# A transformer program on one core: a new table of TensorE's side jobs, and the transposed probabilities fetched by three DMAs of 12 blocks instead of two of 18

## The reference, cut to what matters

```python
# third layer: causal attention, 32 query heads, 8 key/value heads, head size 64, rope
xq = (x @ wq).reshape(Bx, Tx, N_HEAD, HEAD_DIM)
xk = (x @ wk).reshape(Bx, Tx, N_KV_HEAD, HEAD_DIM)
xv = (x @ wv).reshape(Bx, Tx, N_KV_HEAD, HEAD_DIM)
xq = xq * cos + _rotate_half(xq) * sin
xk = xk * cos + _rotate_half(xk) * sin
scores = jnp.einsum('bqhd,bkhd->bhqk', xq, xk) * scale
scores = jnp.where(causal[None, None], scores, -jnp.inf)
probs = jax.nn.softmax(scores, axis=-1)
out = jnp.einsum('bhqk,bkhd->bqhd', probs, xv)
return out.reshape(Bx, Tx, N_HEAD * HEAD_DIM) @ wo
```

## Time and profile before

| | |
|---|---|
| median of 2 runs | 609.65 us (608.51 to 610.8) |
| the profiled execution: its own time | 610.31 us |
| the profiled execution: its span, first to last instruction | 608.5 us |
| granted TensorE clock, mean over the span | 0.992 |
| PE busy | 557.9 us (92%) |
| ACT busy | 436.8 us (72%) |
| DVE busy | 458.2 us (75%) |
| POOL busy | 452.5 us (74%) |
| share of the 16 DMA engines taken by the hardware queue of SP | 82.1% |

### The profile page before, as it was taken

How to read it: one execution, slowest core, us unless ns; L and a number is a source line. 1 busy time by engine, 2 the same in 40 slices (tenths; PEclk the granted TensorE clock), 3 DMA queues, 4 the chain that set the end, 5 groups by cost and what they waited for, 6 DMA issues and landing times.

```text
span 608.5 us, 16334 instructions
## 1 busy us (share of the span) xinstructions
PE 557.9 (92%) x6880; PEld 481.3 (79%) x6880; DVE 458.2 (75%) x751; ACT 436.8 (72%) x608; POOL 452.5 (74%) x371
## 2 busy tenths in 40 slices
PE   5999999987879999999989999999999997996898
PEld 4878898976767898888878888888888976885666
DVE  4686766777767888887877877788788875675897
ACT  0524401249688889889788988988988888974876
POOL 3034426447998998999899899899999977874423
PEclk9999999999999999999999999999999999997989
DMA  8160004006999999999999999999999999998001
GB/s 283 62 209 0 2 21 83 11 2 138 183 175 194 193 183 195 194 199 196 180 181 198 219 196 195 181 212 184 196 177 210 197 184 203 190 177 158 1 27 44
DMA packets 317193, 91.76 MB, mean 151 GB/s; under 512 B 305984, under 2 KB 316224, under 8 KB 317120
## 3 DMA queue, kind: packets, MB, share of 16 engines
q1 hardware_dynamic: 311680, 86.66, 82.1%
q10 hardware_dynamic: 5440, 4.06, 2.6%
HBM read 13.11 MB, written 1.05 MB: 23 GB/s over the span
## 4 chain that ended last, share of the span: by engine, by line
PE 41%; POOL 18%; DVE 16%; DMA 11%; ACT 6%; SPq 4%; issue 4%; POOLq 0%; ACTq 0%; DVEq 0%
POOL p_lo L501 13%; PE PS L1278 12%; DMA pT_lo<-p_lo 10%; PE PS L1537 7%; DVE small L1097 6%; PE PS L1557 4%; PE PS L1411 3%; SPq L402 3%; ACT probs L715 2%; POOL roped L490 2%; PE PS L1388 2%; PE PS L1393 2%; PE PS L1389 2%; PE PS L1301 2%; PE PS L1561 2%
## 5 line engine op out<-in xcount | busy, mean ns | idle before, releaser
L501 POOL TENSOR_TENSOR p_lo<-probs,p_hi 128x2048 f16<-128x2048 f32 (+7 forms) x128 | 303.6, 2390 | 34.4 <-DMA pT_lo<-p_lo 18.8
L715 ACT ACTIVATE probs<-PS,small 128x128 f32<-128x128 f32 (+7 forms) x256 | 173.5, 743 | 43.7 <-DVE small L1097 41.6
L1097 DVE TENSOR_REDUCE small<-PS 128x2 f32<-128x2048 f32 (+7 forms) x128 | 172.8, 1351 | 21.4 <-PE PS L1537 20.9
L724 ACT CAST p_hi<-probs 128x2048 f16<-128x2048 f32 (+7 forms) x128 | 145.8, 1160 | 5.0 <-DMA pT_hi<-p_hi 4.9
L1557 PE MATMUL PS<-v_hi,pT_hi 128*128 128x65 f16 x1152 | 78.8, 194 | 1.3 <-DMA pT_hi<-p_hi 1.3
L1561 PE MATMUL PS<-v_lo,pT_hi 128*128 128x64 f16 x1152 | 78.7, 195 | 0.0
L1537 PE MATMUL PS<-k_hi,q_hi 64*128 64x512 f32 (+3 forms) x384 | 74.0, 381 | 2.5 <-ACT probs L715 2.5
L1557 PEld LDWEIGHTS PS<-v_hi,pT_hi 128*128 128x128 f16 x1152 | 73.9, 99 | 3.0 <-issue 1.4
L1561 PEld LDWEIGHTS PS<-v_lo,pT_hi 128*128 128x128 f16 x1152 | 72.5, 98 | 0.5
L1537 PE MATMUL PS<-k_lo,q_hi 64*128 64x512 f32 (+3 forms) x384 | 66.0, 339 | 0.0
L1537 PE MATMUL PS<-k_hi,q_lo 64*128 64x512 f32 (+3 forms) x384 | 66.0, 339 | 0.0
(11 more groups left out here) (210 smaller groups left out, 1349.6 us busy)
## 6 DMA issues: line engine op xcount, KB each, us to landing
wgu_nat<-L_ffn_w_gate_up SPq DMA_DIRECT2D x2, 1024.0 KB, 9.4
wo_nat<-L_attn_wo ACTq DMA_DIRECT2D x7, 256.0 KB, 3.1
wkq_nat<-L_attn_wq ACTq DMA_DIRECT2D x6, 256.0 KB, 5.1
x<-L_attn_x SPq DMA_DIRECT2D x4, 256.0 KB, 3.9
wdn_nat<-L_ffn_w_down SPq DMA_DIRECT2D x1, 1024.0 KB, 11.0
wfc_nat<-L_ffn_w_fc SPq DMA_DIRECT2D x1, 1024.0 KB, 6.7
wpj_nat<-L_ffn_w_proj SPq DMA_DIRECT2D x1, 1024.0 KB, 9.8
pT_hi<-p_hi SPq DMA_TRANSPOSE x64, 5.5
```

The costliest lines, as they stand in the source:

```text
L501: nc.gpsimd.tensor_tensor(p16_lo[G % 2][:, cols], probs[G % 2][:, cols], p16_hi[G % 2][:, cols], ALU.subtract).then_inc(p_lo_done, 1)
L715: nc.scalar.activation(probs[G % 2][:, start:start + w], PS[:, src:src + w], ACT.Exp, bias=nmax[:, 4 * (G % 2) + u:4 * (G % 2) + u + 1]).t ...
L724: nc.scalar.copy(p16_hi[G % 2][:, cols], probs[G % 2][:, cols]).then_inc(p_hi_done, 1)
L1097: nc.vector.tensor_reduce(nmax[:, first:first + 2], both_heads(G, part), AX.X, ALU.max, negate=True).then_inc(nmax_done, 1)
```

## The change

Three things are changed.

1. The two transposes of a step become three. The float16 probabilities of a step, high and low, now lie in one tile p16 of 36 blocks (high in blocks 0 to 17, low in 18 to 35), the transposed ones in one tile pT of 36 blocks. SP transposes blocks 0 to 11, 12 to 23 and 24 to 35 (`turn_third`). The first third waits for the first part of `p_high` alone when that part has at least 12 blocks (it has 10, 12, 14 or 16), else for both; the second waits for both parts of `p_high` and the first of `p_low`; the third for both of `p_low`. `pv` waits for each third as it comes to its first block. `p_high` of part 0 now waits for the first third of two steps before, and if it has more than 12 blocks for the second as well, `p_high` of part 1 for the second; `p_low` of part 0 waits for the second and the third.
2. The tables. JOBS is new in nearly every step. In a step of groups 1 to 6 the rope projections were 1, 2, 2, 2, 1, 0, 0, 0 and become 1, 2, 1, 1, 1, 2, 0, 0; the output projections were in steps 4, 5, 6, 7 and come to 2, 4, 6, 7, in the order 1, 2, 0, 3, and those of the middle tiles (1, 2) wait for three "ot" jobs, not four; "ot0" moves from step 7 to step 5, "kt1" from slot 2 of step 5 to slot 2 of step 6, "q0t1" to slot 0 of step 7. In RAMP_JOBS "q0t0" moves from step 6 to step 5. The wo weights are split at step 1 of every group but the first, not at step 2 (for the groups before the last).
3. Addresses: roped, y and yT_hi move by 1.5 KB, t_sin by 1.5 KB, o32 to other places, to make room for the joined tiles.

The diff, without the hunks of addresses and of the order count `qk_index`:

```diff
...
-    p16_hi = [sb(f"p16_hi{b}", 186 + 9 * b, [18 * P], F16) for b in range(2)]
-    p16_lo = [sb(f"p16_lo{b}", 190.5 + 9 * b, [18 * P], F16) for b in range(2)]
-    pT_hi = [sb(f"pT_hi{b}", kb, [18, P], F16) for b, kb in enumerate((26, 30.5, 104.5))]
-    pT_lo = [sb(f"pT_lo{b}", kb, [18, P], F16) for b, kb in enumerate((60, 128, 132.5))]
-    o32 = [sb(f"o32{b}", kb, [4, HEAD], F32) for b, kb in enumerate((109.5, 110.5, 78, 79))]
+    p16 = [sb(f"p16_{b}", 186 + 9 * b, [36 * P], F16) for b in range(2)]
+    p16_hi = [t[:, 0:18 * P] for t in p16]
+    p16_lo = [t[:, 18 * P:36 * P] for t in p16]
+    pT = [sb(f"pT_{b}", kb, [36, P], F16) for b, kb in enumerate((26, 128, 104.5))]
...
 
         scores_done, nmax_done, exp_done = sem("scores_done"), sem("nmax_done"), sem("exp_done")
         p_hi_done, p_lo_done = sem("p_hi_done"), sem("p_lo_done")
-        pT_hi_landed = [sem(f"pT_hi_landed{b}") for b in range(3)]
-        pT_lo_landed = [sem(f"pT_lo_landed{b}") for b in range(3)]
+        pT_landed = [[sem(f"pT_third{k}_landed{b}") for b in range(3)] for k in range(3)]
         pv_done, recip_done, norm_done = sem("pv_done"), sem("recip_done"), sem("norm_done")
         oT_done, oT_hi_done, oT_lo_done = sem("oT_done"), sem("oT_hi_done"), sem("oT_lo_done")
         wo_done = sem("wo_done")
...
 
             return {NT - 2: 0, NT - 1: 2}.get(t, 4)
 
+        THIRD = 12
+
+        def third_landed(k, G):
+
+            return pT_landed[k][G % 3], 16 * (G // 3 + 1)
+
         def q_tile(G, part):
             return blocks(G, part) - 1
 
...
 
 
         RAMP_JOBS = {0: ("", "v6", "v7"), 1: ("q1t0", "q1t1", "r0"), 2: ("r1", "r2", ""), 3: ("r3", "r4", ""),
-                     4: ("kt0", "r5", "r6"), 5: ("", "r7", ""), 6: ("kt1", "q0t0", "q0t1"), 7: ("ot0", "", "ot1")}
-        JOBS = {0: ("q1t0", "q1t1", "r0"), 1: ("r1", "r2", "ot2"), 2: ("r3", "r4", ""), 3: ("ot3", "r5", "r6"),
-                4: ("kt0", "wo0", "r7"), 5: ("", "wo1", "kt1"), 6: ("q0t0", "wo2", "q0t1"), 7: ("ot0", "wo3", "ot1")}
+                     4: ("kt0", "r5", "r6"), 5: ("q0t0", "r7", ""), 6: ("kt1", "", "q0t1"), 7: ("ot0", "", "ot1")}
+        JOBS = {0: ("q1t0", "r0", "q1t1"), 1: ("r1", "r2", "ot2"), 2: ("r3", "wo1", ""), 3: ("", "r4", "ot3"),
+                4: ("kt0", "wo2", "r5"), 5: ("ot0", "r6", "r7"), 6: ("q0t0", "wo0", "kt1"), 7: ("q0t1", "wo3", "ot1")}
 
         LAST_JOBS = {0: ("q1t0", "q1t1", ""), 1: ("", "", "ot2"), 2: ("", "", ""), 3: ("ot3", "wo1", ""),
                      4: ("wo2", "", ""), 5: ("ot0", "wo0", ""), 6: ("wo3", "", ""), 7: ("ot1", "po1", "po2")}
-        LAST_WO = (1, 2, 0, 3)
+        WO_ORDER = (1, 2, 0, 3)
         TAIL_TILES = (2, 3, 4, 5, 0, 1, 6, 7)
 
         def wo_count(gg, j):
 
-            return 4 * gg + (LAST_WO.index(j) if gg >= NG - 2 else j) + 1
+            return 4 * gg + WO_ORDER.index(j) + 1
 
         def owner(G, name):
 
...
             load_wkq(1)
             sp.wait_ge(ternT_landed, 32)
 
-            def transpose_hi(G):
-                sp.wait_ge(p_hi_done, 2 * G + 2)
-                sp.dma_start(pT_hi[G % 3][:], p16_hi[G % 2][:], transpose=True).then_inc(pT_hi_landed[G % 3], 16)
-
-            def transpose_lo(G):
-                sp.wait_ge(p_lo_done, 2 * G + 2)
-                sp.dma_start(pT_lo[G % 3][:], p16_lo[G % 2][:], transpose=True).then_inc(pT_lo_landed[G % 3], 16)
+            def turn_third(G, k):
+                sp.dma_start(pT[G % 3][:, THIRD * k:THIRD * (k + 1), :], p16[G % 2][:, THIRD * k * P:THIRD * (k + 1) * P],
+                             transpose=True).then_inc(pT_landed[k][G % 3], 16)
 
             for G in range(STEPS):
                 if G >= 3:
                     sp.wait_ge(pv_done, G - 2)
-                transpose_hi(G)
-                transpose_lo(G)
+                sp.wait_ge(p_hi_done, 2 * G + (1 if 2 * blocks(G, 0) >= THIRD else 2))
+                turn_third(G, 0)
+                sp.wait_ge(p_hi_done, 2 * G + 2)
+                sp.wait_ge(p_lo_done, 2 * G + 1)
+                turn_third(G, 1)
+                sp.wait_ge(p_lo_done, 2 * G + 2)
+                turn_third(G, 2)
 
             for t in range(NT):
                 sp.wait_ge(result_done, t + 1)
...
                 cols = slice(sl.start * P, sl.stop * P)
                 pool.wait_ge(p_hi_done, 2 * G + part + 1)
                 if G >= 2 and part == 0:
-                    pool.wait_ge(pT_lo_landed[(G - 2) % 3], 16 * ((G - 2) // 3 + 1))
+                    pool.wait_ge(*third_landed(1, G - 2))
+                    pool.wait_ge(*third_landed(2, G - 2))
                 nc.gpsimd.tensor_tensor(p16_lo[G % 2][:, cols], probs[G % 2][:, cols], p16_hi[G % 2][:, cols],
                                         ALU.subtract).then_inc(p_lo_done, 1)
 
...
                 p_low(G, 0)
                 if n == 5 and g + 2 < NG:
                     split_wkq_low(g + 2)
-                if n == (1 if g == NG - 1 else 2) and g:
+                if n == 1 and g:
                     split_wo_low(g - 1)
                 if n == 3 and g == NG - 1:
                     split_wo_low(g)
...
                 cols = slice(sl.start * P, sl.stop * P)
                 act.wait_ge(exp_done, 4 * G + 2 * part + 2)
                 if G >= 2 and part == 0:
-                    act.wait_ge(pT_hi_landed[(G - 2) % 3], 16 * ((G - 2) // 3 + 1))
+                    act.wait_ge(*third_landed(0, G - 2))
+                if G >= 2 and (part or sl.stop > THIRD):
+                    act.wait_ge(*third_landed(1, G - 2))
                 nc.scalar.copy(p16_hi[G % 2][:, cols], probs[G % 2][:, cols]).then_inc(p_hi_done, 1)
 
             split_wkq_high(0)
...
                     load_wkq(g + 2)
                 if n == (0 if g == NG - 1 else 4):
                     load_wo(g)
-                if n == (1 if g == NG - 1 else 2) and g:
+                if n == 1 and g:
                     split_wo_high(g - 1)
                 if n == 3 and g == NG - 1:
                     split_wo_high(g)
...
 
             def pv(G, b):
 
-                g, buf, turn = G // 8, G % 3, G // 3 + 1
+                g, buf = G // 8, G % 3
                 o = bank(b)
                 first = True
-                for pT, landed in ((pT_hi, pT_hi_landed), (pT_lo, pT_lo_landed)):
-                    pe.wait_ge(landed[buf], 16 * turn)
+                for low in range(2):
                     for part in range(2):
                         n, c = blocks(G, part), part_cols(G, part).start
                         for a in range(2):
                             u = (2 * part + a) * (HEAD + 1)
                             for j in range(n):
-                                p_block = pT[buf][:, c + a * n + j, :]
+                                at = 18 * low + c + a * n + j
+                                if at % THIRD == 0:
+                                    pe.wait_ge(*third_landed(at // THIRD, G))
+                                p_block = pT[buf][:, at, :]
                                 last = nc.tensor.matmul(o[:, u:u + HEAD + 1], p_block, v_hi[:, j, g, :], start=first,
                                                         stop=False, skip_group_check=True)
                                 first = False
-                                if pT is pT_hi:
+                                if not low:
                                     nc.tensor.matmul(o[:, u:u + HEAD], p_block, v_lo[:, j, g * HEAD:(g + 1) * HEAD],
                                                      start=False, stop=False, skip_group_check=True)
                 last.then_inc(pv_done, 1)
...
             def out_project(gg, j, b):
 
                 pe.wait_ge(wo_split, gg + 1)
-                pe.wait_ge(oT_lo_done, 4 * gg + (2 if gg == NG - 1 and j in (1, 2) else 4))
+                middle = 2 if gg == NG - 1 else 3
+                pe.wait_ge(oT_lo_done, 4 * gg + (middle if j in (1, 2) else 4))
                 hi, lo = wo_hi[gg // (NG - 1)], wo_lo[gg // (NG - 1)]
                 for t in (2 * j, 2 * j + 1):
                     tok = slice(t * P, (t + 1) * P)
```

More of the change, by code:

```diff
@@ L111, in transformer_program @@
     t_cos = [sb(f"t_cos{b}", 35 + 1.25 * b, [5, HEAD], F32) for b in range(2)]
-    t_sin = [sb(f"t_sin{b}", 124 + 1.25 * b, [5, HEAD], F32) for b in range(2)]
-    roped = sb("roped", 112, [NT, 3 * P], F32)
+    t_sin = [sb(f"t_sin{b}", 125.5 + 1.25 * b, [5, HEAD], F32) for b in range(2)]
+    roped = sb("roped", 113.5, [NT, 3 * P], F32)
     k_hi = [sb(f"k_hi{b}", 138 + 8 * b, [T], F32R) for b in range(2)]
@@ L119, in transformer_program @@
     probs = [sb(f"probs{b}", 51 - 9 * b, [18 * P], F32) for b in range(2)]
-    p16_hi = [sb(f"p16_hi{b}", 186 + 9 * b, [18 * P], F16) for b in range(2)]
-    p16_lo = [sb(f"p16_lo{b}", 190.5 + 9 * b, [18 * P], F16) for b in range(2)]
-    pT_hi = [sb(f"pT_hi{b}", kb, [18, P], F16) for b, kb in enumerate((26, 30.5, 104.5))]
-    pT_lo = [sb(f"pT_lo{b}", kb, [18, P], F16) for b, kb in enumerate((60, 128, 132.5))]
```

(13 more changed lines are left out.)

## The result

The changed kernel takes 632.31 us (629.26 to 635.36, two runs) against 609.65 us, a ratio of 1.038 with a 95% interval of 1.029 to 1.048. The forecast was 611.5 us in a range of 600 to 624 us: the time came out 20.8 us above it, outside the range, and for a reason that the forecast does not have. The profiled execution took 635.36 us, with a span of 633.5 us and a mean granted clock of 0.968; before it was 0.992.

A forecast was written before the change was run, and what follows sets the result against it. The prediction took the full SP queue of transposes to bound the kernel from step 12 on, with PE's chain just as long. It summed 610.31 + 5.8 - 4.0 = 612.1 us profiled, so 611.5 us, range 600 to 624 us.

The forecast's parts named there:

- The tables: Term for moved jobs: same work on PE, DVE, ACT and POOL, only bank release times change; taken at nothing.
- At most that is won, at worst as much is lost: 10.8 us either way: Bound on the tables' term, from PE's 1.8 us idle in group 4, over six groups.
- 0.09 us for an additional DMA: Cost term: spacing less data time, 2.83 - 2.74 us, once more in each of 64 steps, 5.8 us.
- From above: Upper bound on an additional DMA, from transposes of 16 and 18 blocks: 0.31 us each, 19.8 us in all.
- From below: at best the three need only their bytes: Lower bound on the DMA term: 5.49 us against 5.66 us, a gain of 0.17 us a step or 10.9 us.
- The second rival: A transpose has a fixed cost of 0.31 us in its start on the queue: 625 us, chance 0.14.
- So from step 12 to the end the transposes are a full queue: Bound on the SP queue: 5.66 us a step undisturbed and about 0.8 us of pauses, against 6.46 us.
- PE's chain is just as long: Claim that PE's chain equals the queue's step, since in groups meeting few pauses the queue has small holes.
- The first rival: Queue only looks full, PE's chain sets the step; table wins 5.4 us, holes 5 us: 599 us, chance 0.26.
- Earlier starts: Gain term: thirds waiting for fewer parts fill holes in SP's queue; 4 of 5.0 us counted, -4 us.
- `p_high` of part 0 is released later: Term for ACT's rounding needing the second third, 0.94 us later; taken at nothing, as covered by the queue.
- third rival: Later release of `p_high`: eight waits grow by 0.94 us, 7.5 us: 619 us, chance 0.10; sign: waits over 8 us.

The follow-up runs named there:

- the table alone: Changed kernel with the old two transposes of 18 blocks, keeping the new table, its split at step 1 and its waits: 630.48 us, ratio 1.031.
- PE kept busy through it: Changed kernel with 50 small matmuls put ahead of PE's wait for the wo split in groups 1 to 6: 623.87 us, ratio 1.022.
- the split at step 0: Changed kernel with wo split at step 0, not 1 (last group unchanged): 607.22 us, 0.993; the same with two transposes of 18 blocks: 609.77 us, 0.999.
- the projection in step 3: Changed kernel with the first output projection moved from slot 1 of step 2 to slot 0 of step 3, split left at step 1: 606.58 us, 0.993.
- four DMAs: Kernel with the first output projection in step 3, with four transposes of 9 blocks a step instead of three of 12: 613.68 us, ratio 1.006.
- halves: Kernel with the first output projection in step 3, with the old two transposes of 18 blocks instead of three of 12: 611.04 us, ratio 1.001.
- thirds and the old table: Changed kernel with the old tables, old place of the split and old output projection waits, three transposes kept: 609.25 us, ratio 0.998.

## Why the prediction was wrong, point by point

**"The tables. The count of jobs is unchanged ... I take nothing".** This is the step that failed. It priced the moved jobs by the free banks and by the load of each engine in each step, and the wo split only as 1.3 us of POOL's time. It did not ask who reads what the split makes. The reader was moved from step 4 to step 2 in the same table, the maker from step 2 to step 1, and POOL is at its step 1 while PE is at its step 2 and later. "At most that is won, at worst as much is lost: 10.8 us either way" was no bound, since it came from PE's idle time before and a new wait has nothing to do with that. The runs: PE waits 3.1 us in each of six groups, the table alone loses 3.1%, and the split one step earlier takes all of it away. The text counted how far the queue runs behind POOL, as cover for a late POOL, and never how far POOL runs behind PE. No rival named the wait either.

**The clock.** Not in the forecast. In group 3 of the changed kernel the wait of 3.09 us is followed by 5.8 us at 0.50, and PE kept busy through it stays at 1.00: 10.9 us of the loss in the profiled execution. The Trainium skill, TensorE: Matmul & The Clock Gate, "Why this matters for your kernels", warns of idle gaps between bursts of matmuls, because TensorE comes out of them at its lower clock. This case agrees in the main: 0.50 behind the gap, 1.00 with the gap filled; but three of the six such gaps of the table alone left the clock at 1.00.

**0.09 us for an additional DMA, "5.8 us, all of it on a full queue".** The spacing was right (1.90 us measured, 1.92 forecast), the conclusion from it was not. On the same table three transposes beat two, by 0.5% (0.9933 / 0.9986) with the split at step 0 and by 0.7% with the projection in step 3. The fixed part that I took, 2.83 - 2.74 us, is a small difference of two large numbers, and three measured together, 5.70 us, are level with the two, 5.66 us. A DMA that adds so little costs time only where the queue sets the step: the third did not, the fourth did.

**"From above", 0.31 us, and "From below: at best the three need only their bytes".** Both were lines through two sizes, and the cost is not one line. The transpose of 6 blocks shows 0.42 us above its bytes, that of 12 blocks 0.07 us: near 1.33 us there seems to be a floor, and above it the bytes set the pace. Only one size lies at that floor, so its shape is a reading. 12 blocks are above the floor. The second rival ("a real fixed cost on the queue, in its start") was right for a size that the change does not use. The Trainium skill, DMA: Bandwidth & Descriptors, "Anatomy of one DMA", has about 2.0 us of fixed cost per DMA, for the path from GpSimd; no size here paid that on the queue, and 1.33 us for 6 blocks is data and all.

**"So from step 12 to the end the transposes are a full queue", and "PE's chain is just as long".** Half right. The queue was nearly without holes before. POOL's waits for transposes, in the kernel before and with thirds and the projection in step 3:

```profile
POOL p_lo L501 <- DMA pT_lo<-p_lo: 18.8, 17, 2.9
```

```profile
POOL p L509 <- DMA pT<-p: 2.6, 2, 1.3
```

They nearly vanished, but the groups went only from 310.2 to 309.1 us (310.7 us with the split at step 0), so the queue was not what made them long by much. The first rival, the queue that only looks full, was nearer here, though its 5.4 us from the table did not come. What sets the step in its place, PE's chain (295.2 of 309.1 us busy) or POOL's (294.6), no run tells apart. With four DMAs the queue does become full. In one pair of profiles it decides more in the last group, 46.9 us before, 46.6 us with halves and 45.1 us with thirds; the other pair does not show that.

**"Earlier starts", -4 us.** The whole gain of thirds over halves, 0.2% with the old table (an interval that reaches no change) and 0.5 to 0.7% with the repaired ones (3 to 4 us), is no larger than the 4 us that I had for the starts alone; the part of the data and that of the starts were not told apart.

**"`p_high` of part 0 is released later."** Taken at nothing, and the time bears that out, but not the waits. The changed kernel has 2.9 us of them against 4.9 us, with a queue that PE's own waits had emptied. With thirds and the old table they did grow, past the 8 us that the prediction gave as the sign of its third rival:

```profile
ACT p L733 <- DMA pT<-p: 10.6, 10, 2.3
```

That kernel was no slower for it (0.998), so these waits were covered.

**The sum.** 610.31 + 5.8 - 4.0 had two terms of the queue, and measured they come out at -1 to -4 us together instead of +1.8. The term of the tables was put at 0; it is 630.48 - 611.31 = 19.2 us by the table alone, and the six groups of the changed kernel are 27.0 us longer in its profile.

## What to carry to other kernels

When a job is moved in a hand-written order, list for each thing it reads the engine that makes it, the place of that in the maker's own order, and how far that engine is behind; the load by step says nothing of it. A wait that leaves TensorE idle for some 3 us can cost more than its length, since slow matmuls can follow it: here 10.9 us beside 16.1 us. And before counting DMAs as so many fixed costs, measure the size at which they stop following their bytes.

## What the runs showed of the hardware that I had not expected

The granted clock fell to 0.50 at an idle stretch of 3.1 us in every one of groups 1 to 6 of the changed kernel, and in three of six in the table alone, which has the same wait. What a fall cost differed too, 1.4 to 2.6 us a group, so a kernel with such a wait can vary from one execution to the next (635.36 and 629.26 us here). It did not fall where PE had 50 small matmuls in the gap. Nor is a wait of 3 us needed: with the split at step 0 the clock falls in the last group, 0.7 us behind the end of an idle stretch of 1.68 us, and with the projection in step 3 a stretch of the same length (up to 509.16 us) left it at 1.00. The rows with the split at step 0:

```profile
511.12 0.28 PE L1533 MATMUL PS<-masked,picked 128*128 128x128 bf16 x2 [1.68 <-ACT probs L723]
```

```profile
511.80:515.30 3.50, 3.50 (x28) 2.86 (x25) 1.76 (x1) 1.90 (x3) 3.50 (x3) 0.51 1.16 221
```

The pauses of all transfers that the prediction reads in the earlier trace rows recur, and each of the two looked at begins right behind a packet of 16,384 bytes on an instruction queue: such packets start at 300.3 and 306.8 us in the kernel before, and from 300.8 to 302.0 us 7 GB/s move, from 307.2 to 308.4 us 6 GB/s. That the one makes the other is not shown.

DMA transposes from one queue seem to have a floor: those of 6 blocks (196,608 bytes) followed each other no faster than one in 1.33 us, where their bytes at 215 GB/s are 0.91 us. With 384 of them the kernel took 742.9 us, with 192 of 12 blocks, which move the same bytes, 607.2 us.
